# Attention of a fused layer kernel: value sums in a bank of their own, squares a step later, and a new order of input, normalisation and key copies

## The chip, the cores and the metric

One core of a Trainium2 chip runs the kernel. The metric is the device time of one execution in microseconds (us), the median of the runs shown. PE is TensorE, ACT ScalarE, DVE VectorE, POOL GpSimd, SP SyncE.

## The reference

Input is `x` of 64 sequences of 64 tokens with 256 features, and a condition vector of 64 numbers per sequence. Four layers follow each other, all in float32:

```python
x = _L0_cond_ref(x, cond_256, ...)   # conditioned RMS norm, gated GELU, quantised down projection, + x
x = _L1_cond_ref(x, cond_256, ...)   # attention with 16 heads, then SwiGLU
x = _L2_cond_ref(x, cond_256, ...)   # adapter with weights generated per sequence
x = _L3_cond_ref(x, cond_256, ...)   # layer norm with a conditioned bias
```

The change is in the attention half of the second layer:

```python
x = x + a_alpha * _attention(_ada_rmsnorm(x, t, gamma_w, beta_w), W_q, W_k, W_v, W_o)
# _ada_rmsnorm: gamma * x * rsqrt(mean(x * x) + EPS) + beta
attn = softmax(scale * einsum('bnqd,bnkd->bnqk', q, k))
o = einsum('bnqk,bnkd->bnqd', attn, v)
```

## The kernel before

Features lie on the partitions. Float32 products are made of three passes over a high and a low part (`SPLITS`, L45): ACT copies a tensor into its high part, POOL or DVE subtracts that from the tensor to get the low part. Attention works on NA = 16 tiles of 256 tokens (4 sequences). It is a software pipeline written out by hand: each engine has an `attention_body(s)` that is called for step t = s.t, and its parts work on the tile t minus a lag (`s.at(lag)`): lag 0 is the input of the projections, 1 the projections, 2 scores and softmax, 3 the transposed probabilities and the weighted values, 4 the output projection and residual. Engines run ahead of each other only as far as the semaphores `A[...]` let them; on each engine the order of the calls is the order of the work.

`pipeline` (L78) writes out the steps up to t = 8 (`PEELED`, L849), runs t = 9 to 14 in a loop, two steps per turn, and writes out t = 15 and, except on POOL, 16. `plain(s)` (L940) is true from step 9 on, `before_plain(s)` (L944) from step 8 on. Steps 1 to 3 on PE are written out apart from the body (from L1381 on, `a1` to `a3`), as are the last ones, `d0` to `d3` (steps 16 to 19). In the first steps the tail of the first layer still runs in between.

What each engine does in a step, with the names used below:

- **POOL** (L1058): the input in parts (`attention_input`, L169): part 0 multiplies x by its rstd (L182), part 1 multiplies gamma (L186) and adds beta (L188), part 2 subtracts the high part to make the low part (L191); the residual (L1056), which adds the scaled output of lag 4 to x; two normalisations (L1047), which multiply the exponentials by the reciprocal of their sums. In steps up to 8 the order is part 0, 1, 2, residual, norm, norm (in step 3 one norm stands ahead of part 2). From step 9 on it is part 1, residual, part 2, norm, norm, part 0 of the next step; step 8 also ends with part 0 of step 9.
- **PE** (L1286): scores (L1215), first transposes (L1237), output projection (L1281), second transposes (L1237), squares (L1266, only for the first four tiles), keys and queries (both L1156), weighted values (L1254), values (L1191). Transposes wait for the normalisations of the step before. Values go to bank 0 in steps 1 and 2 and from step 8 on, and otherwise share bank 1 with the keys; there they wait for ACT's key copies (`k_done`). The output projection writes bank 0.
- **ACT** (L1500): value copies (L1465 to L1469; in steps up to 8 two of four, the other two are DVE's), copies of the transposes (L1448) and exponentials (L1440) in turn, the high part of the input (L198), key copies (L1476, two per step), query copy (L1485), high part of the attention output (L1491), `rstd` (L1456, L1459) and `square` (L1498) for the first four tiles. The key copies stand behind the high part and the second exponential, but in step 3.
- **DVE** (L1681): value copies (L1670, L1671) in steps up to 8, maxima (L1643) and subtraction (L1647) twice, the scaled output (L1678; from step 9 on between the two pairs), sums (L1655) and reciprocals (L1658) twice, low part of the attention output (L1664).

The squares of the first four tiles give the rstd rows that the SwiGLU part needs first. `square` works at lag 4 at the end of ACT's step, PE's `squares` and ACT's `rstd` at lag 5 in the next one.

Of the kernel before, what the change touches and what calls it, by code (L numbers as in the profile page):

```python
# [831 lines left out]
def layers(nc, io, core, bank, keep, early, adapter_w, base_w, slot_loaded, out):  # L832
# [5 lines left out]
    GTA = GT1  # L838
# [13 lines left out]
    with ExitStack() as c:  # L852
# [73 lines left out]
            return rows.rearrange("p (n b) (g e f) -> p b e n g f", b=2, e=2, f=HD)[:, member, parity]  # L926

        def value_sums(s, member, parity):
            rows = bank[0 if s.first_tile(2) or s.first_tile(3) or plain(s) else 1][L * member:L * (member + 1), :]
            return rows.rearrange("p (n g e f) -> p e n g f", n=2, e=2, f=HD)[:, parity]  # L930

        def pair_of(ap, two):
# [7 lines left out]
        def plain(s):  # L940

            return not isinstance(s.t, int) or s.t > PEELED
# [3 lines left out]
            return not isinstance(s.t, int) or s.t >= PEELED  # L946

        def vector_takes_values(s):
            return not plain(s) or s.last(2)

        def rows_live(s):

# [88 lines left out]
        def _(pool):  # L1041
# [8 lines left out]
            def residual(s):  # L1050
                if s.live(4):
                    t = s.at(4)
                    xt = x[:, :, bass.ds(t * GTA, GTA)]
                    pool.wait_ge(A["ya_done"], t + 1)
                    hold(pool, A["passed"])
                    nc.gpsimd.tensor_tensor(xt, xt, ya1[:], ALU.add).then_inc(A["x_done"], 1)  # L1056

            def attention_body(s):  # L1058
                following = Step(s.t + 1, s.k + 1, NA, s.turns)
                if s.live(0):  # L1060
                    if not plain(s):
                        attention_input(nc, pool, core, s, 0)
                    attention_input(nc, pool, core, s, 1)
                    if s.first_tile(4):
                        first["row_scales"](pool, e35)
                    if plain(s):
                        residual(s)
                    if s.first_tile(3):
                        normalise(s, 0)
                    wait(pool, A["v_ready"], s.at(1) if s.live(2) else 0)  # L1070
                    attention_input(nc, pool, core, s, 2)
                    if not plain(s):
                        residual(s)
                if not s.first_tile(3):
                    normalise(s, 0)
                normalise(s, 1)
                if before_plain(s) and following.live(0):
                    attention_input(nc, pool, core, following, 0)

            def generator_base():  # L1080
                pool.wait_ge(A["base_loaded"], 32)
# [67 lines left out]
        def _(pe):  # L1149
# [19 lines left out]
            def keys(s):  # L1169
                if s.live(1):  # L1170
                    pe.wait_ge(A["h_ready"], s.at(1) + 1)
                    if s.first_tile(3):
                        pe.wait_ge(A["k_done"], s.at(1))
                    elif s.live(2):
                        pe.wait_ge(A["v_low_done"], s.at(1))
                        pe.wait_ge(A["v_high_done"], s.at(1))
                    project(s, W1_K, bank[1], "k_ready")

            def values(s):

                if not s.live(1):
                    return
                k, apart = s.slot(1, 2), s.first_tile(1) or s.first_tile(2) or before_plain(s)
                if before_plain(s):
                    pe.wait_ge(A["ya_done"], s.at(4) + 1)
                elif not apart:
                    pe.wait_ge(A["k_done"], s.at(1) + 1)
                for pair in range(2):
                    for n, (a, b) in enumerate(SPLITS):
                        for d in range(DH):  # L1190
                            last = nc.tensor.matmul(bank[0 if apart else 1][:, pair * D:(pair + 1) * D],  # L1191
                                                    ha[a][k][:, d, pair * P:(pair + 1) * P],
                                                    w1[b][:, W1_V + d * D:W1_V + (d + 1) * D],
                                                    start=n == d == 0, stop=n == 2 and d == DH - 1)
                last.then_inc(A["v_ready"], 1)
# [74 lines left out]
            def output(s):  # L1270
                if s.live(4):
                    ps = output_ps(s)
                    pe.wait_ge(A["ot_done"], s.at(4) + 1)
                    if plain(s) and not s.last(3) and not s.last(4):
                        pe.wait_ge(A["v_low_done"], s.at(2) + 1)
                        pe.wait_ge(A["v_high_done"], s.at(2) + 1)
                    wait(pe, A["ya_done"], s.at(4))
                    for m in range(DH):
                        for n, (a, b) in enumerate(SPLITS):
                            for d in range(2):  # L1280
                                last = nc.tensor.matmul(ps[:, m * GTA:(m + 1) * GTA],  # L1281
                                                        w1[a][:, W1_O + d * D + m * P:W1_O + d * D + (m + 1) * P], ot[b][:, d, :],
                                                        start=n == d == 0, stop=n == 2 and d == 1)
                    last.then_inc(A["o_ready"], 1)

            def attention_body(s):  # L1286
                scores(s)
                transposes(s, 0)
                output(s)
                transposes(s, 1)  # L1290
                squares(s)
                keys(s)
                queries(s)
                weighted_values(s)
                if s.first_tile(4):
                    pe.wait_ge(A["sub_done"], PAIRS * s.at(2) + 1)
                    first["row_lines"](pe, e36)
                values(s)
# [136 lines left out]
        def _(act):  # L1435
# [55 lines left out]
                    nc.scalar.activation(ot[0][:], weighted_ps(s), ACT.Copy).then_inc(A["ot_hi_done"], 1)  # L1491

            def square(s):
                if early(s, 4):
                    act.wait_ge(A["x_done"], s.at(4) + 1)
                    wait(act, A["ss_ready"], s.at(4))
                    hold(act, A["passed"])
                    nc.scalar.activation(sq[:], x[:, :, bass.ds(s.at(4) * GTA, GTA)], ACT.Square).then_inc(A["sq_done"], 1)  # L1498

            def attention_body(s):  # L1500
                take_values(s)
# [6 lines left out]
                exponentials(s, 0)  # L1508
                first_two = s.first_tile(3) or s.first_tile(4)
                take_transposed(s, 1)  # L1510
                if first_two:
                    exponentials(s, 1)
                if s.first_tile(3):
                    take_queries(s)
                if s.live(0):
                    wait(act, A["v_ready"], s.at(1) if s.live(2) else 0)
                    attention_input_high(nc, act, core, s.at(0), s.slot(0, 2))
                if not first_two:
                    exponentials(s, 1)
                if not s.first_tile(3):  # L1520
                    take_keys(s)
                    take_queries(s)
                output_high(s)
                if s.first_tile(4):
                    first["take_lines"](act, e37)
                rstd(s)
                square(s)

            def gate(s, f):
                u = s.at(1) * FC + f  # L1530
# [655 lines left out]
```

## Time and profile before

| | us |
|---|---|
| median of 3 runs (lowest, highest) | 741.57 (741.37, 742.21) |
| the profiled execution | 741.11 |
| its span, first to last instruction | 739.3 |
| busy: PE, DVE, POOL, ACT | 721.8, 514.7, 410.6, 359.3 |
| attention part, on PE's timeline | about 226 to 391 |

The profile is one execution. Times in it count from the start of its span. The granted TensorE clock is 0.998 of full over the whole span. A timeline row has the start in us, the duration in us, engine, line, operation, out<-in, shape, count, and in brackets how long the engine was idle before it and what released it. A row x2 covers two instructions back to back. The end of an instruction overlaps the start of the next by some hundredths, so the distance of two starts is the cost of one.

### The profile page before, as it was taken

How to read it: one execution, taken by the hardware profiler on the slowest of the kernel's cores; microseconds unless marked ns; L12 is line 12 of the kernel's file. 1: busy time of each engine (PE TensorE's matmuls, PEld its weight loads, DVE VectorE, ACT ScalarE, POOL GpSimd, SP SyncE). 2: the span in 40 equal slices, each digit the busy share in tenths (PEclk: the TensorE clock that was granted, in tenths of full speed). 3: DMA queues.
4: the chain of work that ended last, by engine and by line, in shares of the span. 5: the costliest groups of instructions: out<-in, count | busy, mean ns of one | idle time of the engine just before them, and what ended most of it. 6: DMA issues, size and time to landing. Idle time of an engine off the chain costs nothing.

```text
span 739.3 us, 18704 instructions
## 1 busy us (share of the span) xinstructions
PE 721.8 (98%) x6700; PEld 586.4 (79%) x6700; DVE 514.7 (70%) x808; ACT 359.3 (49%) x722; POOL 410.6 (56%) x408
## 2 busy tenths in 40 slices
PE   9999999999999899999999999999999999999996
PEld 8888888888888788888888777777777767778884
DVE  4977777777789989888995465656655566453466
ACT  4534444344447677888874333333333332322585
POOL 5645655554678888999997624224242423320244
PEclk9999999999999999999999999999999999999999
DMA  8854544445432000000004255577667777759943
GB/s 301 258 111 99 108 121 101 100 111 121 110 73 63 22 28 17 17 1 0 1 4 134 104 173 175 177 220 216 191 190 251 212 215 231 238 160 390 386 178 142
DMA packets 81339, 106.25 MB, mean 144 GB/s; under 512 B 39904, under 2 KB 53376, under 8 KB 81152
## 3 DMA queue, kind: packets, MB, share of 16 engines
q1 hardware_dynamic: 79840, 103.34, 46.7%
q10 hardware_dynamic: 1440, 2.11, 1.1%
q8 instruction: 39, 0.64, 0.4%
q14 instruction: 20, 0.16, 0.1%
HBM read 75.77 MB, written 21.27 MB: 131 GB/s over the span
## 4 chain that ended last, share of the span: by engine, by line
PE 75%; POOL 16%; issue 5%; DVE 3%; ACT 1%; DMA 0%; POOLq 0%; DVEq 0%; SPq 0%; ACTq 0%
PE banks L446 24%; PE banks L1317 22%; PE banks L1347 12%; POOL p_sb L1047 5%; PE banks L1369 4%; PE banks L530 4%; POOL mlp_in L182 2%; PE banks L1979 2%; PE banks L1949 2%; POOL mlp_in L186 2%; POOL x_sb L1056 2%; POOL att_in_lo L191 1%; PE banks L1971 1%; POOL mlp_in L188 1%; PE banks L548 1%
## 5 line engine op out<-in xcount | busy, mean ns | idle before, releaser
L629 ACT ACTIVATE gelu<-banks,rstd 128x512 f32<-128x512 f32 x64 | 44.0, 688 | 115.8 <-PE banks L446 114.1
L1699 DVE TENSOR_TENSOR g<-banks,silu 128x512 f32<-128x512 f32 x64 | 44.2, 690 | 77.6 <-PE banks L1317 44.9
L1703 DVE TENSOR_TENSOR g_lo<-g,g_hi 128x512 fp32r<-128x512 f32 x64 | 55.7, 870 | 47.6 <-ACT g_hi L1539 47.6
L1539 ACT ACTIVATE g_hi<-g 128x512 fp32r<-128x512 f32 x64 | 40.4, 631 | 96.0 <-DVE g L1699 95.0
L1533 ACT ACTIVATE silu<-banks 128x512 f32<-128x512 f32 x64 | 38.2, 597 | 97.4 <-PE banks L1317 97.4
L446 PE MATMUL banks<-up_hi,xs_hi 128*128 128x512 f32 x254 | 81.1, 400 | 0.0
L446 PE MATMUL banks<-up_hi,xs_lo 128*128 128x512 f32 x256 | 79.2, 391 | 0.0
L1317 PE MATMUL banks<-mlp_in_hi,w_hi 128*128 128x512 f32 x252 | 78.8, 394 | 0.0
L446 PE MATMUL banks<-up_lo,xs_hi 128*128 128x512 f32 x256 | 78.8, 390 | 0.0
L1317 PE MATMUL banks<-mlp_in_lo,w_hi 128*128 128x512 f32 x252 | 78.0, 390 | 0.0
L1317 PE MATMUL banks<-mlp_in_hi,w_lo 128*128 128x512 f32 x252 | 77.8, 390 | 0.0
L745 DVE SCALAR_TENSOR_TENSOR h<-banks,rstd,gelu 128x512 f32<-128x512 f32 x64 | 47.8, 747 | 37.0 <-ACT gelu L629 37.0
L822 POOL TENSOR_TENSOR mlp_in_lo<-mlp_in,mlp_in_hi 128x1024 fp32r<-128x1024 f32 x8 | 19.9, 2490 | 80.7 <-ACT mlp_in_hi L829 80.7
L1047 POOL TENSOR_TENSOR p_sb<-p_sb,rec 128x1024 f32<-128x1024 f32 x32 | 60.4, 1906 | 5.2 <-DVE rec L1658 5.2
L446 PEld LDWEIGHTS banks<-up_hi,xs_lo 128*128 128x128 f32 x256 | 48.1, 188 | 10.4
L446 PEld LDWEIGHTS banks<-up_lo,xs_hi 128*128 128x128 f32 x256 | 48.1, 188 | 10.2
L1317 PEld LDWEIGHTS banks<-mlp_in_lo,w_hi 128*128 128x128 f32 x252 | 47.3, 188 | 10.7
L1317 PEld LDWEIGHTS banks<-mlp_in_hi,w_hi 128*128 128x128 f32 x252 | 47.2, 188 | 10.8
L1317 PEld LDWEIGHTS banks<-mlp_in_hi,w_lo 128*128 128x128 f32 x252 | 47.3, 188 | 10.2
L1347 PE MATMUL banks<-g_hi,w_hi 128*128 128x512 f32 x128 | 52.6, 411 | 0.7 <-DVE g_lo L1703 0.7
L446 PEld LDWEIGHTS banks<-up_hi,xs_hi 128*128 128x128 f32 x254 | 45.4, 188 | 8.3 <-issue 0.2
L1347 PE MATMUL banks<-g_hi,w_lo 128*128 128x512 f32 x128 | 50.6, 395 | 0.0
(230 smaller groups left out, 1736.2 us busy)
## 6 DMA issues: line engine op xcount, KB each, us to landing
gen_hyper<-in_gen_t SPq DMA_DIRECT2D x32, 512.0 KB, 4.4
gen_made<-base_w SPq DMA_DIRECT2D x64, 256.0 KB, 4.4
adapter_w<-gen_made SPq DMA_DIRECT2D x64, 256.0 KB, 4.4
tokens<-in_x_tok SPq DMA_DIRECT2D x32, 128.0 KB, 2.3
w_stage<-in_w_t SPq DMA_DIRECT2D x32, 128.0 KB, 2.6
tokens_again<-in_x_tok SPq DMA_DIRECT2D x32, 128.0 KB, 2.2
weight_slot<-adapter_w SPq DMA_DIRECT2D x4, 1024.0 KB, 8.8
x_sb<-in_x_t SPq DMA_DIRECT2D x7, 512.0 KB, 6.3
```

The costliest lines, as they stand in the source:

```text
L446: last = nc.tensor.matmul(up_bank(s, j, part)[:, :], (xs_hi, xs_lo)[a][:, k, d, :], up[b][:, d, at:at + 512], start=start and d == 0, stop ...
L530: last = nc.tensor.matmul(y_ps, qt[:, s.slot(2, 2), f, :], downq[:, f, :], start=f == 0, stop=f == FC - 1)
L629: nc.scalar.activation(gelu[:, j, :], up_bank(s, j, 1)[:, :], ACT.Gelu, scale=rstd0[:, bass.ds(s.at(0), 1)]).then_inc(Z["gelu_done"], 1)
L745: nc.vector.scalar_tensor_tensor(out=h[:, k, j * 512:(j + 1) * 512], in0=up_bank(s, j, 0)[:, :], scalar=rstd0[:, bass.ds(t, 1)], in1=gelu[ ...
L1047: nc.gpsimd.tensor_tensor(pu, pu, rec[:, two, :].unsqueeze(2).to_broadcast([P, 16, L]), ALU.mult).then_inc(A["norm_done"], 1)
L1317: last = nc.tensor.matmul(chunk_bank(s, f, i)[:, :], w1[a][:, at:at + P], hs[b][k][:, d, :], start=n == d == 0, stop=n == 2 and d == DH - 1)
L1347: last = nc.tensor.matmul(bank[5 + m][:, :], w1[a][:, at:at + P], gs[b][:, f % 2, :], start=f == n == 0, stop=f == FC - 1 and n == 2)
L1369: last = nc.tensor.matmul(ps[B * half:B * (half + 1), :], scaled[rows, :], hyper[rows, k, half, :], start=True, stop=True)
L1533: nc.scalar.activation(silu[:, f % 2, :], chunk_bank(s, f, 0)[:, :], ACT.Silu).then_inc(S["silu_done"], 1)
L1539: nc.scalar.activation(gs[0][:, f % 2, :], g[:, f % 2, :], ACT.Copy).then_inc(S["g_hi_done"], 1)
L1699: nc.vector.tensor_tensor(g[:, f % 2, :], chunk_bank(s, f, 1)[:, :], silu[:, f % 2, :], ALU.mult).then_inc(S["g_done"], 1)
L1703: nc.vector.tensor_tensor(gs[1][:, f % 2, :], g[:, f % 2, :], gs[0][:, f % 2, :].bitcast(FP32), ALU.subtract).then_inc(S["g_ready"], 1)
```

## The change

Four things. (1) Values always go to bank 0. They wait for the scaled output of lag 4 (from step 4 on), and in steps 2 and 3 for the value copies of the tile before; keys wait for the key copies of the tile before and no longer for value copies; the output projection now waits for the value copies in steps 4 to 8 too. From step 3 on ACT makes all four value copies (DVE keeps its two in step 2 and in the last one). (2) `square` moves to lag 5 and to the place behind ACT's second transposed copy; on PE `squares` moves behind the queries. (3) On ACT, from step 9 on, the key copies stand ahead of the high part of the input. (4) On POOL the residual stands ahead of part 2 in steps 5 to 8 as well; in step 3 both norms stand ahead of part 2, in step 4 the first norm ahead of it and the second behind it, ahead of the residual; from step 8 on, part 0 of the next step stands between the two norms.

```diff
--- before.py
+++ after.py
@@ -926,7 +926,7 @@
             return rows.rearrange("p (n b) (g e f) -> p b e n g f", b=2, e=2, f=HD)[:, member, parity]
 
         def value_sums(s, member, parity):
-            rows = bank[0 if s.first_tile(2) or s.first_tile(3) or plain(s) else 1][L * member:L * (member + 1), :]
+            rows = bank[0][L * member:L * (member + 1), :]
             return rows.rearrange("p (n g e f) -> p e n g f", n=2, e=2, f=HD)[:, parity]
 
         def pair_of(ap, two):
@@ -946,7 +946,7 @@
             return not isinstance(s.t, int) or s.t >= PEELED
 
         def vector_takes_values(s):
-            return not plain(s) or s.last(2)
+            return s.first_tile(2) or s.last(2)
 
         def rows_live(s):
 
@@ -1057,25 +1057,31 @@
 
             def attention_body(s):
                 following = Step(s.t + 1, s.k + 1, NA, s.turns)
+                first_two = s.first_tile(3) or s.first_tile(4)
                 if s.live(0):
                     if not plain(s):
                         attention_input(nc, pool, core, s, 0)
                     attention_input(nc, pool, core, s, 1)
                     if s.first_tile(4):
                         first["row_scales"](pool, e35)
-                    if plain(s):
+                    if not first_two:
                         residual(s)
+                    if first_two:
+                        normalise(s, 0)
                     if s.first_tile(3):
-                        normalise(s, 0)
+                        normalise(s, 1)
                     wait(pool, A["v_ready"], s.at(1) if s.live(2) else 0)
                     attention_input(nc, pool, core, s, 2)
-                    if not plain(s):
+                    if s.first_tile(4):
+                        normalise(s, 1)
+                    if first_two:
                         residual(s)
-                if not s.first_tile(3):
+                if not first_two:
                     normalise(s, 0)
-                normalise(s, 1)
                 if before_plain(s) and following.live(0):
                     attention_input(nc, pool, core, following, 0)
+                if not first_two:
+                    normalise(s, 1)
 
             def generator_base():
                 pool.wait_ge(A["base_loaded"], 32)
@@ -1169,26 +1175,24 @@
             def keys(s):
                 if s.live(1):
                     pe.wait_ge(A["h_ready"], s.at(1) + 1)
-                    if s.first_tile(3):
+                    if s.live(2):
                         pe.wait_ge(A["k_done"], s.at(1))
-                    elif s.live(2):
-                        pe.wait_ge(A["v_low_done"], s.at(1))
-                        pe.wait_ge(A["v_high_done"], s.at(1))
                     project(s, W1_K, bank[1], "k_ready")
 
             def values(s):
 
                 if not s.live(1):
                     return
-                k, apart = s.slot(1, 2), s.first_tile(1) or s.first_tile(2) or before_plain(s)
-                if before_plain(s):
+                k = s.slot(1, 2)
+                if s.live(4):
                     pe.wait_ge(A["ya_done"], s.at(4) + 1)
-                elif not apart:
-                    pe.wait_ge(A["k_done"], s.at(1) + 1)
+                elif s.live(2):
+                    pe.wait_ge(A["v_low_done"], s.at(1))
+                    pe.wait_ge(A["v_high_done"], s.at(1))
                 for pair in range(2):
                     for n, (a, b) in enumerate(SPLITS):
                         for d in range(DH):
-                            last = nc.tensor.matmul(bank[0 if apart else 1][:, pair * D:(pair + 1) * D],
+                            last = nc.tensor.matmul(bank[0][:, pair * D:(pair + 1) * D],
                                                     ha[a][k][:, d, pair * P:(pair + 1) * P],
                                                     w1[b][:, W1_V + d * D:W1_V + (d + 1) * D],
                                                     start=n == d == 0, stop=n == 2 and d == DH - 1)
@@ -1271,7 +1275,7 @@
                 if s.live(4):
                     ps = output_ps(s)
                     pe.wait_ge(A["ot_done"], s.at(4) + 1)
-                    if plain(s) and not s.last(3) and not s.last(4):
+                    if not s.last(3) and not s.last(4):
                         pe.wait_ge(A["v_low_done"], s.at(2) + 1)
                         pe.wait_ge(A["v_high_done"], s.at(2) + 1)
                     wait(pe, A["ya_done"], s.at(4))
@@ -1288,9 +1292,9 @@
                 transposes(s, 0)
                 output(s)
                 transposes(s, 1)
-                squares(s)
                 keys(s)
                 queries(s)
+                squares(s)
                 weighted_values(s)
                 if s.first_tile(4):
                     pe.wait_ge(A["sub_done"], PAIRS * s.at(2) + 1)
@@ -1491,11 +1495,11 @@
                     nc.scalar.activation(ot[0][:], weighted_ps(s), ACT.Copy).then_inc(A["ot_hi_done"], 1)
 
             def square(s):
-                if early(s, 4):
-                    act.wait_ge(A["x_done"], s.at(4) + 1)
-                    wait(act, A["ss_ready"], s.at(4))
+                if early(s, 5):
+                    act.wait_ge(A["x_done"], s.at(5) + 1)
+                    wait(act, A["ss_ready"], s.at(5))
                     hold(act, A["passed"])
-                    nc.scalar.activation(sq[:], x[:, :, bass.ds(s.at(4) * GTA, GTA)], ACT.Square).then_inc(A["sq_done"], 1)
+                    nc.scalar.activation(sq[:], x[:, :, bass.ds(s.at(5) * GTA, GTA)], ACT.Square).then_inc(A["sq_done"], 1)
 
             def attention_body(s):
                 take_values(s)
@@ -1508,23 +1512,26 @@
                 exponentials(s, 0)
                 first_two = s.first_tile(3) or s.first_tile(4)
                 take_transposed(s, 1)
+                square(s)
                 if first_two:
                     exponentials(s, 1)
                 if s.first_tile(3):
                     take_queries(s)
+                if plain(s):
+                    take_keys(s)
                 if s.live(0):
                     wait(act, A["v_ready"], s.at(1) if s.live(2) else 0)
                     attention_input_high(nc, act, core, s.at(0), s.slot(0, 2))
                 if not first_two:
                     exponentials(s, 1)
+                if not plain(s) and not s.first_tile(3):
+                    take_keys(s)
                 if not s.first_tile(3):
-                    take_keys(s)
                     take_queries(s)
                 output_high(s)
                 if s.first_tile(4):
                     first["take_lines"](act, e37)
                 rstd(s)
-                square(s)
 
             def gate(s, f):
                 u = s.at(1) * FC + f
```

## Rows read from the trace of the kernel before

**Rows 1.** The page's chain that ended last, share of the span by engine.

```profile
PE 75%; POOL 16%; issue 5%; DVE 3%; ACT 1%; DMA 0%; POOLq 0%; DVEq 0%; SPq 0%; ACTq 0%
```

**Rows 2.** Windows: length, busy PE, PEld, DVE, ACT, POOL (instructions), clock, DMA.

```profile
...
280.00:290.70 10.70, 10.19 (x226) 9.22 (x225) 9.68 (x13) 8.34 (x15) 9.68 (x9) 1.00 0.09 28
...
331.20:341.20 10.00, 9.61 (x210) 8.79 (x209) 8.80 (x10) 7.99 (x14) 9.62 (x9) 1.00 0.00 0
...
```

**Rows 3.** Timeline of POOL, steps 3 to 6.

```profile
...
245.82 1.91 POOL L1047 TENSOR_TENSOR p_sb<-p_sb,rec 128x1024 f32<-128x1024 f32 x1
...
258.84 1.28 POOL L182 TENSOR_TENSOR mlp_in<-x_sb,stat 128x512 f32<-128x512 f32 x1
...
269.46 1.28 POOL L182 TENSOR_TENSOR mlp_in<-x_sb,stat 128x512 f32<-128x512 f32 x1
...
273.86 1.30 POOL L191 TENSOR_TENSOR mlp_in_lo<-mlp_in,mlp_in_hi 128x512 fp32r<-128x512 f32 x1 [0.87 <-ACT mlp_in_hi L198]
...
```

**Rows 4.** Timeline of POOL, one step of the loop.

```profile
...
332.71 1.04 POOL L186 TENSOR_TENSOR mlp_in<-mlp_in,cond_vectors 128x512 f32<-128x512 f32 x1 [0.20 <-POOL mlp_in L182]
333.94 1.05 POOL L188 TENSOR_TENSOR mlp_in<-mlp_in,cond_vectors 128x512 f32<-128x512 f32 x1 [0.19 <-POOL mlp_in L186]
334.95 1.32 POOL L1056 TENSOR_TENSOR x_sb<-x_sb,y_alpha 128x512 f32 x1
336.23 1.29 POOL L191 TENSOR_TENSOR mlp_in_lo<-mlp_in,mlp_in_hi 128x512 fp32r<-128x512 f32 x1
337.47 3.77 POOL L1047 TENSOR_TENSOR p_sb<-p_sb,rec 128x1024 f32<-128x1024 f32 x2
341.19 1.29 POOL L182 TENSOR_TENSOR mlp_in<-x_sb,stat 128x512 f32 x1
...
```

**Rows 5.** Timeline of PE, starts of groups of matmuls.

```profile
...
220.41 0.48 PE L1156 MATMUL banks<-mlp_in_hi,w_hi 128*128 128x256 f32 x2
...
247.87 0.71 PE L1237 MATMUL banks<-ident,p_sb 64*128 64x64 f32 x16 [0.73 <-POOL p_sb L1047]
...
277.44 1.21 PE L1215 MATMUL banks<-k_sb,q_sb 32*64 32x128 f32 x64
...
286.50 0.51 PE L1191 MATMUL banks<-w_hi,mlp_in_hi 128*128 128x256 f32 x2 [0.51 <-ACT k_sb L1476]
...
371.65 0.71 PE L1237 MATMUL banks<-ident,p_sb 64*128 64x64 f32 x16
...
372.29 0.50 PE L1156 MATMUL banks<-att_in_hi,w_hi 128*128 128x256 f32 x2
...
377.81 1.21 PE L1215 MATMUL banks<-k_sb,q_sb 32*64 32x128 f32 x64
...
```

**Rows 6.** Timeline of ACT.

```profile
...
222.11 1.26 ACT L1476 ACTIVATE k_sb<-banks,vecs 128x512 f32<-128x512 f32 x2 [0.82 <-PE banks L1156]
...
273.08 0.63 ACT L198 ACTIVATE mlp_in_hi<-mlp_in 128x512 fp32r<-128x512 f32 x1 [0.49 <-POOL mlp_in L188]
...
336.51 1.25 ACT L1476 ACTIVATE k_sb<-banks,vecs 128x512 f32<-128x512 f32 x2
337.65 0.60 ACT L1485 ACTIVATE q_sb<-banks 128x512 f32<-128x512 f32 x1
...
338.60 0.38 ACT L1465 ACTIVATE v_sb<-banks 64x256 f32<-64x256 f32 x1
...
```

**Rows 7.** Timeline of DVE, step 7.

```profile
...
278.68 1.22 DVE L1643 TENSOR_REDUCE mx<-banks 128x16 f32<-128x1024 f32 x1 [0.26 <-PE banks L1215]
...
283.46 0.68 DVE L1678 TENSOR_TENSOR y_alpha<-banks,cond_vectors 128x512 f32<-128x512 f32 x1
...
285.30 0.25 DVE L1658 RECIPROCAL rec<-rsum 128x16 f32<-128x16 f32 x1
...
```

**Rows 8.** Timeline of POOL, ends of steps 8 and 15.

```profile
...
297.61 3.77 POOL L1047 TENSOR_TENSOR p_sb<-p_sb,rec 128x1024 f32<-128x1024 f32 x2
...
370.83 2.38 POOL L812 TENSOR_TENSOR mlp_in<-x_sb,stat 128x1024 f32<-128x1024 f32 x1
...
```

## The prediction

> **What bounds the kernel now.** Read the chain of waits first: PE holds 75% of it, POOL 16% [rows 1]. POOL's share all lies in the attention part, 226 to 391 us, so that part is read by windows: in a step of the loop POOL is busy 9.62 of 10.00 us and PE 9.61, DVE and ACT 8.80 and 7.99; in an early step POOL is at 9.68 of 10.70 and PE at 10.19 [rows 2]. Then the timeline of POOL. An early step takes 269.46 - 258.84 = 10.62 us, and 0.87 of it is POOL waiting for ACT's high part of the input before it can subtract the low part [rows 3]. In the loop the residual stands in that hole; what is left is 0.20 before gamma and 0.19 before beta, each waiting for the instruction just ahead on POOL [rows 4]. From the end of the second normalisation of step 8 (297.61 + 3.77 = 301.38) to the start of the SwiGLU input (370.83) lie seven steps, 69.45 us, 9.92 each [rows 8]. Behind that point POOL is on the chain until PE takes over, and everything later follows, so a shift there goes to the end of the kernel whole.
>
> **The change, part by part.** Write E(t) for the end of the second normalisation of step t, T1(t) for PE's second transposes, S(t) for its scores.
>
> *Steps 3 and 4.* Two value copies leave DVE for ACT, where they are of the kind in [rows 6] (0.38 us, some 0.39 apart); the maxima start about 0.9 earlier, with scores already there, and reciprocals and normalisations follow. I take 0.88. The first two norms now run ahead of low part and residual; POOL's work is only reordered, so the input of step 5 starts at 258.84 - 0.88 = 257.96 [rows 3]. PE gains more (its transposes and keys no longer stand behind the low part): T1(5) about 257.3.
>
> *Steps 5 to 8.* The residual covers the 0.87 hole, so POOL alone would need 10.62 - 0.9 = 9.72. But PE was busy 10.19 of 10.70 [rows 2], its hole being the 0.51 before the values, which waited for the key copies [rows 5]. Values in bank 0 lose that wait; squares only change place. PE then needs 10.1. At the turn to step 6 it pays once more. ACT starts the high part when beta ends (261.5), and with the exponential (1.0), key copies (1.14) and query copy its queries are there some 3.3 later, 264.8, where PE could take scores at 263.9: 0.9. Then high output, two rstd activations and four value copies run to 267.4, and the output matmuls, which write that bank, could have gone at 266.7: 0.7. So T1(6) = 257.3 + 10.1 + 1.6 = 269.0 and, with ACT now ahead, T1(7) = 279.1. Scores follow T1 by 377.81 - 371.65 = 6.16 [rows 5], with the squares 6.5; the scaled output ends 1.24 + 5.46 us after the scores start (277.44, 278.68, 283.46 + 0.68) [rows 5, 7]. So S(8) = 285.7, the scaled output of step 8 is there at 292.4, and POOL goes on without a hole: residual 1.28, low part 1.24, first norm 1.86, next input 1.28 (taken like the residual, same form), second norm 1.9 [rows 4]: E(8) = 300.0, 1.4 earlier than 301.38.
>
> *Steps 9 to 14, the loop.* Here POOL's order becomes gamma, beta, residual, low, norm, next input, norm. On POOL by itself this is a gain: the second norm stands between the next input and gamma, and about 0.2 of the 0.4 us of gaps goes, 9.92 to 9.73. What is pushed back is T1: it waits for the second norm, which now ends 1.28 later in the step. And ACT now copies the keys ahead of the high part. Keys on PE stand behind T1. So a loop of one step closes, all links from rows without cover:
> - second norm to T1: 247.87 - 245.82 = 2.05 (PE had waited for it) [rows 3, 5];
> - T1 to keys 0.64 [rows 5];
> - keys to the first key copy 222.11 - 220.41 = 1.70 (ACT had waited) [rows 5, 6];
> - two key copies 337.65 - 336.51 = 1.14 [rows 6];
> - high part to low part 273.86 - 273.08 = 0.78 (POOL had waited) [rows 3, 6];
> - low part 1.24, first norm 3.72 / 2 = 1.86, next input 1.28 [rows 4].
>
> The sum is 10.69 us per step against 9.92. Of the parts, keys first costs nothing while T1 is early (T1 lay 0.7 before gamma), nor does the moved input while keys come last; the cover of each is what the other takes. Put on POOL's clock: keys are copied by E + 3.6 and the high part by E + 4.3, where POOL wants it at E + 3.5. Six such steps are 64.14, and step 15 has no next input, 10.69 - 1.28 = 9.41: 73.55 against 69.45, a loss of 4.1. No register wait or loop branch is added that the loop of before does not have; I bound the sum of links between 10.4 (each hand-over 0.05 shorter, as POOL to ACT looks in the loop) and 10.9 (each 0.03 longer).
>
> *Free of cost.* DVE's two copies less per early step (it is not the bound); keys' wait for the value copies gone, replaced by one for the older key copies; the square one step later: it is read only by squares that already ran in that step, and waits for a residual of the step before. If ACT were full there, its 0.6 would delay the high part; it has over 1 us idle. No DMA is moved; rstd rows leave in the same step as before.
>
> Sum: -1.4 + 4.1 = +2.7 on the profiled execution's own 741.11 (span 739.30 and 1.8 around it), 743.8. The median of the runs is 741.57, 0.46 above that execution; on the median: **744.2**.
>
> **A rule against this.** By occupancy POOL and PE share the top of a loop step at 9.6 of 10.0 [rows 2]. The Trainium skill (Perfetto Trace Analysis, Identifying the Most-Contended Engine) says the engine with the highest occupancy is the one to improve, and the change does fill POOL's gaps. The row agrees about who is fullest; it does not say what fills the step once the order changes. Followed by itself, that rule gives rival 1.
>
> **Rivals.**
> 1. *Faster: the key copies do not hold the high part.* If keys were ready early enough, the next bound of the loop is a cycle over two steps: norm to T1 2.05, T1 to scores 6.16, to maxima 1.24, maxima to reciprocal's end 285.30 + 0.25 - 278.68 = 6.87, 0.07, norm 1.86, input 1.28 = 19.5, so 9.8 each [rows 4, 5, 7]. Then 6 x 9.8 + 8.5 = 67.3, 2.1 less than 69.45, with the 1.4: -3.5, 738.1. It decides at (69.45 + 1.4 + 1.28) / 7 = 10.3 us per loop step: below, faster; above, slower. For it: both saturated engines gain slack. Against: links measured without cover sum to 10.69.
> 2. *PE does not bind in steps 5 to 8*: E(8) = 257.96 + 4 x 9.72 + 1.28 = 298.1, 3.3 gained: +0.8, 742.4. Against it PE's 10.19 busy.
> 3. *No gain in steps 5 to 8*, since ACT's 0.76 of copies hold the output matmuls each step: 10.62 stays, E(8) = 301.7: +4.4, 746.0.
> 4. The reordering is hidden throughout, 741.6.
>
> **How the numbers follow.** Forecast 0.52 (its own range 743.0 to 745.4), rival 1 0.24, rival 2 0.11, rival 3 0.10, rival 4 0.03. A measurement of this kernel tells about 0.2% (1.5 us) from nothing, so rivals 2 and 4 are "same": 0.14. Faster is rival 1, 0.24; slower is forecast and rival 3, 0.62. The range takes forecast, 2, 3 and 4, which is 0.76, and the upper half of rival 1 (loop steps between 9.9 and 10.2): 738.8 to 746.6.
>
> **What the changed profile would show.** POOL's 0.87 hole of steps 5 to 8 gone and PE's wait for key copies before the values too; in the loop the gap before gamma gone, a new POOL wait of 0.8 to 1.0 before the low part, released by ACT's high part, with the key copies just ahead of it on ACT; T1 waiting on POOL; PE idle about 1.1 per step; loop steps 10.7 apart; the SwiGLU input starting at 373.5. I am wrong in the main point if loop steps are under 10.3 apart or that wait is missing; only in size, if E(8) is off 300.0.

## Result and profile after

The changed kernel takes 747.11 us (median of 5, 746.34 to 747.35) against 742.14 for the kernel before on the same chip (median of 5): ratio 1.0073 [1.0062, 1.0085], 5.0 us slower. The forecast was 744.2, in a range of 738.8 to 746.6, or +2.6 on its before (741.57): the side was right, the size 2.4 short. The measured loss added to the forecast's own before would make 746.5, just inside that range.

The page's busy times and its chain by engine, after. POOL's share falls from 16% [rows 1] to 11% and "issue" rises to 8%:

```profile
PE 723.2 (97%) x6700; PEld 587.9 (79%) x6700; DVE 506.4 (68%) x796; ACT 365.9 (49%) x734; POOL 410.4 (55%) x408
...
PE 75%; POOL 11%; issue 8%; DVE 3%; ACT 1%; DMA 0%; POOLq 0%; DVEq 0%; SPq 0%; ACTq 0%
```

The time went in two places, and the timeline of POOL shows both. Each L182 row starts the input of a step (3, 4, 5, 6, 7, 8); 300.68 is the second norm of step 8, 376.27 the SwiGLU input:

```profile
237.78 1.29 POOL L182 TENSOR_TENSOR mlp_in<-x_sb,stat 128x512 f32<-128x512 f32 x1
...
242.54 3.77 POOL L1047 TENSOR_TENSOR p_sb<-p_sb,rec 128x1024 f32<-128x1024 f32 x2 [1.23 <-DVE rec L1665]
...
247.70 1.29 POOL L182 TENSOR_TENSOR mlp_in<-x_sb,stat 128x512 f32<-128x512 f32 x1
...
258.85 1.31 POOL L182 TENSOR_TENSOR mlp_in<-x_sb,stat 128x512 f32<-128x512 f32 x1
...
268.58 1.28 POOL L182 TENSOR_TENSOR mlp_in<-x_sb,stat 128x512 f32<-128x512 f32 x1
...
274.31 1.31 POOL L1056 TENSOR_TENSOR x_sb<-x_sb,y_alpha 128x512 f32<-128x512 f32 x1 [2.21 <-ACT mlp_in_hi L198]
...
280.53 1.31 POOL L182 TENSOR_TENSOR mlp_in<-x_sb,stat 128x512 f32<-128x512 f32 x1
...
290.92 1.28 POOL L182 TENSOR_TENSOR mlp_in<-x_sb,stat 128x512 f32<-128x512 f32 x1
...
300.68 1.93 POOL L1047 TENSOR_TENSOR p_sb<-p_sb,rec 128x1024 f32<-128x1024 f32 x1
...
376.27 2.40 POOL L812 TENSOR_TENSOR mlp_in<-x_sb,stat 128x1024 f32<-128x1024 f32 x1
```

Profiled executions reach the attention part at different times (the input of step 3 starts at 237.38 before and 237.78 here, between 236.65 and 238.30 in all), so stretches are compared from that row on. From it to the SwiGLU input, 133.45 us have become 138.49: +5.04, which is the loss in the medians (4.97).

**The loop.** From the end of step 8's second norm, 302.61, to 376.27 are 73.66 us, where before had 69.45. One step, POOL:

```profile
311.41 1.91 POOL L1047 TENSOR_TENSOR p_sb<-p_sb,rec 128x1024 f32<-128x1024 f32 x1
...
315.51 1.31 POOL L1056 TENSOR_TENSOR x_sb<-x_sb,y_alpha 128x512 f32 x1
317.77 1.29 POOL L191 TENSOR_TENSOR mlp_in_lo<-mlp_in,mlp_in_hi 128x512 fp32r<-128x512 f32 x1 [0.96 <-ACT mlp_in_hi L198]
319.02 1.90 POOL L1047 TENSOR_TENSOR p_sb<-p_sb,rec 128x1024 f32<-128x1024 f32 x1
320.88 1.27 POOL L182 TENSOR_TENSOR mlp_in<-x_sb,stat 128x512 f32 x1
322.12 1.90 POOL L1047 TENSOR_TENSOR p_sb<-p_sb,rec 128x1024 f32<-128x1024 f32 x1
```

The timeline of PE and that of ACT in the same step:

```profile
313.47 0.71 PE L1241 MATMUL banks<-ident,p_sb 64*128 64x64 f32 x16 [0.77 <-POOL p_sb L1047]
314.11 0.50 PE L1162 MATMUL banks<-att_in_hi,w_hi 128*128 128x256 f32 x2
```

```profile
315.91 1.27 ACT L1480 ACTIVATE k_sb<-banks,vecs 128x512 f32<-128x512 f32 x2 [0.67 <-PE banks L1162]
317.07 0.63 ACT L198 ACTIVATE mlp_in_hi<-mlp_in 128x512 fp32r<-128x512 f32 x1
```

This is a closed ring: each step waits for the step before through all of the links. POOL's norm, begun at 311.41, lets PE's second transposes go at 313.47 (2.06); keys follow 0.64 later; ACT copies them 1.80 after that, then makes the high part (1.16); POOL's low part starts at 317.77 (0.70), and after low part, norm and input (1.25, 1.86, 1.24) the next second norm starts at 322.12: 10.71. POOL was ready 0.96 before the high part came, where before it had no wait [rows 4].

**Steps 6 to 8.** Step 6 lasts 11.95 (268.58 to 280.53), where before took 10.61. PE and ACT at its start:

```profile
264.13 0.40 PE L1195 MATMUL banks<-w_hi,mlp_in_lo 128*128 128x256 f32 x2
266.56 2.02 PE L1219 MATMUL banks<-k_sb,q_sb 32*64 32x128 f32 x64 [2.03 <-ACT early_rstd L1460]
268.50 1.11 PE L1241 MATMUL banks<-ident,p_sb 64*128 64x64 f32 x16
```

```profile
265.13 0.59 ACT L1489 ACTIVATE q_sb<-banks 128x512 f32<-128x512 f32 x1
265.60 0.60 ACT L1495 ACTIVATE ot_hi<-banks 128x512 fp32r<-128x512 f32 x1
266.08 0.33 ACT L1460 ACTIVATE early_rstd<-banks,wscale 128x64 f32<-128x64 f32 x1
```

The scores write bank 3, where the sums of squares lie until the first rstd activation has read them. ACT comes to that activation only behind key copies, queries and high output, so PE waits on it (`ss_done`). It was no earlier before: 7.20 after the input of step 5 (266.04 - 258.84), now 7.23 (266.08 - 258.85). The same place in the kernel before, ACT and PE:

```profile
266.04 0.33 ACT L1456 ACTIVATE early_rstd<-banks,wscale 128x64 f32<-128x64 f32 x1
```

```profile
265.25 0.50 PE L1191 MATMUL banks<-w_hi,mlp_in_hi 128*128 128x256 f32 x2 [0.69 <-ACT k_sb L1476]
...
266.87 1.21 PE L1215 MATMUL banks<-k_sb,q_sb 32*64 32x128 f32 x64
```

There PE's values had stood for the key copies, and its scores started at 266.87, when the activation was over (266.37). Values in bank 0 no longer stand for them; PE is through with the values at 264.53 and meets what lay hidden behind that wait. The new place of the squares on PE has no part in it: they are done at 262.03, 4 us ahead of the activation. The scores then took 2.02 where 1.21 was usual [rows 5]. A window of both, and the loop step (columns as in [rows 2]):

```profile
266.50:268.60 2.10, 2.04 (x66) 1.74 (x68) 0.43 (x1) 1.66 (x5) 2.10 (x3) 0.50 0.00 0
...
323.98:334.69 10.71, 9.87 (x208) 8.99 (x208) 8.95 (x11) 8.31 (x14) 9.55 (x8) 1.00 0.00 0
```

After the 2.03 us of idle PE was granted 0.50, its 1.2 GHz level, until about 269.9. So the scaled output is late and POOL stands 2.21 before the residual at 274.31. (The row names ACT's high part, which had long been done; DVE's scaled output, 273.45 to 274.13, came last.) PE's largest entry of waits in steps 5 to 8, with the sum, the number and the longest:

```profile
PE banks L1219 <- ACT early_rstd L1460: 3.1, 3, 2.0
```

### The profile page after: what moved, and what is told of

It reads as the page before. It is cut to its first block, busy times and chain, and to the rows that moved or that the text cites. A ratio compares the mean times of both kernels' runs of the same rounds, so it can differ in the third digit from the quotient of the medians.

```text
span 745.3 us, 18706 instructions
## 1 busy us (share of the span) xinstructions
PE 723.2 (97%) x6700; PEld 587.9 (79%) x6700; DVE 506.4 (68%) x796; ACT 365.9 (49%) x734; POOL 410.4 (55%) x408
## 4 chain that ended last, share of the span: by engine, by line
PE 75%; POOL 11%; issue 8%; DVE 3%; ACT 1%; DMA 0%; POOLq 0%; DVEq 0%; SPq 0%; ACTq 0%
PE banks L446 24%; PE banks L1321 22%; PE banks L1351 12%; PE banks L1373 4%; PE banks L530 4%; POOL p_sb L1047 2%; PE banks L1986 2%; PE banks L1956 2%; POOL mlp_in L182 2%; POOL x_sb L1056 2%; POOL mlp_in L186 1%; DVE mx L1650 1%; POOL mlp_in_lo L191 1%; PE banks L1978 1%; PE banks L548 1%
## 5 line engine op out<-in xcount | busy, mean ns | idle before, releaser
L1710 DVE TENSOR_TENSOR g_lo<-g,g_hi 128x512 fp32r<-128x512 f32 x64 | 52.4, 819 | 47.5 <-ACT g_hi L1546 47.5
L1321 PEld LDWEIGHTS banks<-mlp_in_lo,w_hi 128*128 128x128 f32 x252 | 47.3, 188 | 10.7
L1321 PEld LDWEIGHTS banks<-mlp_in_hi,w_lo 128*128 128x128 f32 x252 | 47.3, 188 | 10.3
```

The costliest lines, as they stand in the source:

```text
L1321: last = nc.tensor.matmul(chunk_bank(s, f, i)[:, :], w1[a][:, at:at + P], hs[b][k][:, d, :], start=n == d == 0, stop=n == 2 and d == DH - 1)
L1710: nc.vector.tensor_tensor(gs[1][:, f % 2, :], g[:, f % 2, :], gs[0][:, f % 2, :].bitcast(FP32), ALU.subtract).then_inc(S["g_ready"], 1)
```

## Experiments

Each kernel was timed against the kernel before on its own chip, whose median was 741.44 in the first four, 741.50 in the next four and 741.49 in the last two; beside the changed kernel it was 742.14, so that kernel is compared with them by its distance to before, +5.0. Two theories stood against each other: that the two late edits (next input between the norms, keys first) together close the loop and the early part merely falls short; or that one of them is bad by itself.

### Next input behind both norms

```diff
@@ attention_body (POOL), from the changed kernel
                 if not first_two:
                     normalise(s, 0)
-                if before_plain(s) and following.live(0):
-                    attention_input(nc, pool, core, following, 0)
                 if not first_two:
                     normalise(s, 1)
+                if before_plain(s) and following.live(0):
+                    attention_input(nc, pool, core, following, 0)
```

> Edit: the changed kernel, but on POOL the input of the next step goes back behind both normalisations; keys stay first on ACT. My theory (the loss is a loop of one step: second norm, T1, keys, key copies, high part, low part, norm, input; 10.7 us): with T1 early again the key copies are done before beta ends, keys first costs nothing, loop steps are 9.9 apart, no wait before the low part; the whole 5.4 us of steps 8 to 15 come back, about 741.8, within 0.5 of the kernel before. Rival 'keys first alone holds the high part': steps stay at 10.5 or more, 746 to 747.

741.19, ratio 0.9995 [0.9986, 1.0005]. POOL:

```profile
313.65 1.32 POOL L1056 TENSOR_TENSOR x_sb<-x_sb,y_alpha 128x512 f32 x1
314.92 1.29 POOL L191 TENSOR_TENSOR mlp_in_lo<-mlp_in,mlp_in_hi 128x512 fp32r<-128x512 f32 x1
...
323.60 1.29 POOL L1056 TENSOR_TENSOR x_sb<-x_sb,y_alpha 128x512 f32 x1
```

The wait before the low part is gone and the step is 9.95, though keys are still copied ahead of the high part.

### Keys last on ACT

```diff
@@ attention_body (ACT), from the changed kernel
-                if plain(s):
-                    take_keys(s)
...
-                if not plain(s) and not s.first_tile(3):
-                    take_keys(s)
                 if not s.first_tile(3):
+                    take_keys(s)
                     take_queries(s)
```

> Edit: the changed kernel, but on ACT the key copies go back behind the high part and the second exponential; the input stays between the norms on POOL. My theory: the one-step loop is open, so the next bound holds: POOL alone at 9.73 or the cycle over two steps at 9.8. Steps 9 to 14 at 9.75 to 9.95, the part behind 301 us about 1 us shorter than in the kernel before: 740.3 to 741.5. Rival 'the moved input alone does it, since T1 is pushed back': steps 10.5 or more, 746 to 747.

741.65, ratio 1.0004 [0.9993, 1.0015]. POOL:

```profile
313.23 1.31 POOL L1056 TENSOR_TENSOR x_sb<-x_sb,y_alpha 128x512 f32 x1
...
316.11 1.91 POOL L1047 TENSOR_TENSOR p_sb<-p_sb,rec 128x1024 f32<-128x1024 f32 x1 [0.32 <-DVE rec L1662]
...
323.30 1.30 POOL L1056 TENSOR_TENSOR x_sb<-x_sb,y_alpha 128x512 f32 x1
```

The median is 0.15 above the expected range. With the keys out of the way the waits that are left are where rival 1 put them, on the reciprocals: the norm waits 0.32 for them in this step and 0.22 in the next, and residuals lie 9.72, 10.07 and 9.96 apart (from 303.51), where rival 1 had 9.8.

### Both undone: the early part alone

Both diffs above together.

> Edit: the changed kernel with both late edits undone (input behind both norms, keys last); what is left is the early part: values apart, squares later, the order of steps 3 to 8. My theory as the changed trace now shows it: the early part is worth nothing (end of step 8 at 302.6 less the 1.24 of the moved input is 301.4, as before), so 741.8 plus or minus 0.6, loop steps 9.9. What I predicted of it (1.4 us faster) would give 740.5. Rival 'the early part costs itself, through the waits for rstd': 743 or more.

740.83, ratio 0.9992 [0.9982, 1.0001]: 0.4 under the expected range. So the whole early part is worth 0.6 us, not clear of nothing, and not the 2.6 that the forecast holds for it (step 8 ends 1.4 earlier there although the moved input, 1.28, already stands ahead of its end; the 740.5 of the expectation left the 1.28 out). PE, and a window of its clock:

```profile
265.44 1.20 PE L1219 MATMUL banks<-k_sb,q_sb 32*64 32x128 f32 x64 [2.08 <-ACT early_rstd L1460]
```

```profile
266.50:268.60 2.10, 2.10 (x30) 1.92 (x22) 1.90 (x2) 1.64 (x3) 2.10 (x2) 0.59 0.00 0
```

### The late part alone

The kernel before, with only the two late edits of the change (keys first on ACT in the loop, next input between the norms).

> Edit: the kernel before with the two late edits alone (from step 8 the input between the norms, from step 9 keys first). My theory: 5.4 us slower than before, 747, loop steps 10.7, with a wait of 1.0 before the low part. Rival 'late and early parts hurt together': under 744.

747.23, ratio 1.0074 [1.0058, 1.0091], no different from the changed kernel. POOL:

```profile
315.60 1.31 POOL L1056 TENSOR_TENSOR x_sb<-x_sb,y_alpha 128x512 f32 x1
317.86 1.29 POOL L191 TENSOR_TENSOR mlp_in_lo<-mlp_in,mlp_in_hi 128x512 fp32r<-128x512 f32 x1 [0.95 <-ACT mlp_in_hi L198]
...
326.29 1.31 POOL L1056 TENSOR_TENSOR x_sb<-x_sb,y_alpha 128x512 f32 x1
```

Steps of 10.69 to 10.71 us. The two edits together cost 5.8 us (on top of the early part 5.6: +5.0 less -0.6), each alone nothing that these runs tell (0.4 and 0.8 above the kernel with neither, intervals overlapping): the loop needs both to close. That settles the late part. The next four kernels ask where the early gain went. All start from the kernel with both late edits undone (740.83).

### Squares back at their earlier place

```diff
@@ square (ACT); likewise squares ahead of keys on PE
-                if early(s, 5):
-                    act.wait_ge(A["x_done"], s.at(5) + 1)
+                if early(s, 4):
+                    act.wait_ge(A["x_done"], s.at(4) + 1)
...
                 take_transposed(s, 1)
-                square(s)
...
                 rstd(s)
+                square(s)
```

> Edit, on the kernel with both late edits undone (input and keys last): the square part of the change undone too (ACT squares at lag 4 at the end of its step, PE's squares ahead of the keys). The residual of tile 0 is now the last thing POOL does in step 4 (it ends at 258.9), so the square at the end of ACT's step 4 would hold ACT from 254.5 until then, in front of the value copies of step 5. Theory: this costs 3 to 4.5 us, 744 to 745.5; the later square is what the new order of steps 3 and 4 needs. Rival 'the later square is what costs (it makes the rstd late)': 740 or less.

746.12, ratio 1.0055 [1.0040, 1.0069]: 5.2 worse than with later squares, more than either expectation. ACT and POOL:

```profile
258.68 0.63 ACT L1502 ACTIVATE sq<-x_sb 128x512 f32<-128x512 f32 x1 [4.80 <-POOL x_sb L1056]
```

```profile
267.07 1.31 POOL L1056 TENSOR_TENSOR x_sb<-x_sb,y_alpha 128x512 f32<-128x512 f32 x1 [5.06 <-DVE y_alpha L1682]
```

The residual now stands behind norms in the first steps; a square that still wants that step's residual stops ACT for 4.80, its value copies behind it, and PE's output matmuls stand 5.08 for these. PE was then granted 0.50 from about 260.0 to 266.9, so the 5.2 are that stop and the clock together; step 5 takes 14.80 instead of 9.70. The later squares are no saving of their own but what the new order needs. Nor is their place on PE what makes the scores wait for rstd, since one such wait is left with the squares ahead of the keys:

```profile
292.58 1.20 PE L1219 MATMUL banks<-k_sb,q_sb 32*64 32x128 f32 x64 [0.31 <-ACT early_rstd L1460]
```

### First rstd activation ahead of the high output

```diff
@@ attention_body (ACT); rstd(s, (0,)) is the first activation, (1,) the second
                 square(s)
+                if s.first_tile(5):
+                    rstd(s)
...
+                if not s.first_tile(5):
+                    rstd(s, (0,))
                 output_high(s)
...
-                rstd(s)
+                if not s.first_tile(5):
+                    rstd(s, (1,))
```

> Edit, on the kernel with both late edits undone: ACT's rstd earlier. In step 5 both activations stand right behind the square, where ACT idles 1.85 us; in steps 6 to 8 the first one, the only one that the scores wait for, stands ahead of the high output, the second behind it. Theory (the early gain was lost at scores that wait for the rstd activation which frees their bank, 2.0 to 2.1 us idle at step 6, 0.4 and 0.7 at the next two, and a lower clock behind the first): scores of step 6 start 0.5 earlier, the two later waits go, PE's idle time before the scores is 1.5 and the clock stays up; 1.0 to 2.0 us faster than with both late edits undone, 738.8 to 739.8. Rival 'queries, not rstd, set the scores': under 0.3 us.

739.42, ratio 0.9976 [0.9967, 0.9984]: 1.5 less against before than without it, and faster than both kernels of this study. PE, step 6:

```profile
265.02 1.20 PE L1219 MATMUL banks<-k_sb,q_sb 32*64 32x128 f32 x64 [1.55 <-ACT k_sb L1482]
```

```profile
266.50:268.60 2.10, 2.10 (x28) 1.90 (x27) 2.07 (x2) 1.37 (x2) 2.10 (x2) 1.00 0.00 0
```

The scores' wait on rstd is gone, the one left in step 6 ends with ACT's query copy (264.33 to 264.92; the row names the key copies, done by then), and the clock stays at 1.00. (In step 5 both activations stand right behind the square, where ACT had been idle.)

### Both rstd activations ahead of it

The same, with `rstd(s)` whole ahead of `output_high(s)`.

> Edit, on the kernel with both late edits undone: both rstd activations ahead of the high output in steps 5 to 8. Theory: the scores of step 6 wait for the query copy and one activation, 0.5 less than now, the high output comes 0.6 later and has room: 0.3 to 1.0 faster than with both late edits undone, 739.8 to 740.5. Rival: high output late holds DVE's low part and the maxima, no gain.

741.26, ratio 0.9992 [0.9983, 1.0001]: no gain. PE:

```profile
266.55 1.20 PE L1219 MATMUL banks<-k_sb,q_sb 32*64 32x128 f32 x64 [1.58 <-ACT early_rstd L1460]
268.24 0.72 PE L1241 MATMUL banks<-ident,p_sb 64*128 64x64 f32 x16 [0.50 <-DVE ot_lo L1668]
```

The high output, now 1.08 behind the query copy instead of 0.48, holds DVE's low output and by it PE: 0.50, 0.46 and 0.46 in three steps. The kernel's one profile is shorter than this median says (131.62 from the input of step 3 to the SwiGLU input, against 132.98 without the edit, in a profile with the clock's fall). Part of the rest is the clock: four of its eleven executions have a mean clock of 0.995 and take 741.41 to 742.35; the median of the other seven is 740.44, against 739.33 for the ten of twelve that kept the clock with only the first activation ahead. The two kernels also differ in step 5, so the last 1.1 us isn't split further.

### DVE takes two of the value copies again

```diff
@@ vector_takes_values; steps 3 to 8 split the four copies as before
-            return s.first_tile(2) or s.last(2)
+            return not plain(s) or s.last(2)
```

> Edit, on the kernel with both late edits undone: DVE takes two of the four value copies again in steps 3 to 8. Theory: maxima of step 3 start 0.9 later (what the change gained there, about 0.6 of it real) but ACT's copies end 0.8 earlier, which bounds only the output matmuls (waits of 0.2 in all): 741.0 to 741.6, 0.2 to 0.6 slower than with both late edits undone. Rival 'four copies on ACT are what ate the early gain' (rival 3 of the prediction): 1 us or more faster, under 740.

741.22, ratio 0.9998 [0.9988, 1.0007]. PE:

```profile
266.13 1.20 PE L1219 MATMUL banks<-k_sb,q_sb 32*64 32x128 f32 x64 [2.13 <-ACT early_rstd L1460]
```

With 0.76 us less on ACT the wait is no shorter: rival 3's cause falls. The first norm of step 3 waits 1.82 again and that step is 10.50 long instead of 9.91, so the moved copies are worth 0.6 in that profile, once.

### The rstd repair with the loop open, and with the loop closed

The rstd diff above, on the kernel with keys last alone, and on the changed kernel itself.

> The key copies of the loop stand behind the high part and the exponential again, the next input stays between the norms, and the first rstd activation of steps 6 to 8 runs ahead of the high output (step 5: both behind the square). My theory: the early repair is worth what it was with both late edits undone, about 1.4 us (739.42 against 740.83), and the loop stays open at steps of 9.7 to 10.1 us, so 741.65 - 1.4 = 740.3, range 739.2 to 741.2; scores of step 6 start near 265.0 with the granted clock near 1.00 behind them. Rival: with keys last the loop follows a two-step cycle through the maxima (about 9.9 us a step) that doesn't care when it is entered, so the gain of the early part is swallowed: 741.4 to 741.9.

> The changed kernel whole, with only the first rstd activation of steps 6 to 8 ahead of the high output (step 5: both behind the square). My theory: the early part and the closed loop of the late steps add up, so the repair is worth its 1.4 us here too and the loop still steps by 10.7 us: 747.1 - 1.4 = 745.7, range 744.9 to 746.3, with the SwiGLU input 1.4 to 1.9 us earlier than 376.27. Rival: the early loss was cover for the loop and the loop absorbs an earlier start: 746.8 to 747.4.

The first: 739.69, ratio 0.9978 [0.9969, 0.9987], as fast as the best, so the loop with keys last passes an early gain on. The second: 744.60, ratio 1.0051 [1.0037, 1.0065], +3.1 against before where the changed kernel has +5.0: 1.9 gained (by the traces 138.49 - 136.53 = 1.96), not 1.4. The 744.60 itself is 0.3 under the bottom of my range, which had not allowed for the other chip's before. Its POOL, the end of step 8 and a loop step:

```profile
298.15 1.92 POOL L1047 TENSOR_TENSOR p_sb<-p_sb,rec 128x1024 f32<-128x1024 f32 x1
...
312.96 1.31 POOL L1056 TENSOR_TENSOR x_sb<-x_sb,y_alpha 128x512 f32 x1
...
323.60 1.29 POOL L1056 TENSOR_TENSOR x_sb<-x_sb,y_alpha 128x512 f32 x1
```

Step 8 ends at 300.07, 2.54 before the changed kernel (0.70 of it because its attention began earlier), and the loop still goes by 10.64: the losses of the two parts add up. With the activation in its new place the changed kernel comes near what was forecast for it (+2.6).

## Why the prediction was right in its side and wrong in its size

**The loop, right.** Forecast: steps of 10.69, a wait of 0.8 to 1.0 before the low part on ACT's high part with the key copies just ahead, 1.1 us of PE idle per step, 73.55 us from E(8) to the SwiGLU input. Measured: 10.70 and 10.71, 0.96, 10.71 - 9.87 = 0.84 idle, 73.66. The ring's links were each within 0.10 of the rows that the forecast took them from. That each edit covers for the other was shown by the two kernels that undo one of them. Taking each link only from rows where the receiver had been waiting, so that nothing hid a part of it, held.

**Steps 3 and 4: 0.88 forecast, 0.39 measured** (input of step 5 at 21.46 us after that of step 3 before, 21.07 after). DVE in step 3:

```profile
235.75 1.16 DVE L1650 TENSOR_REDUCE mx<-banks 128x16 f32<-128x1024 f32 x1
237.43 1.23 DVE L1654 TENSOR_TENSOR p_sb<-banks,mx 128x1024 f32<-128x1024 f32 x1 [0.52 <-PE banks L1241]
```

The maxima did start earlier, by 1.0 against the start of attention (236.36 before), but the subtraction then waited 0.52 for PE's second transposes, which still read its buffer; 0.6 reached the norm, and 0.2 of that went between low part and next input. In step 4 POOL had no wait on another engine in either kernel (11.16 and 11.15 us), so nothing could be gained there.

**Steps 5 to 8: the step that failed.** E(8), the end of step 8's second norm, was put 42.04 after the input of step 5; it came after 302.61 - 258.85 = 43.76, which is 1.72 late. With 0.49 and 0.11 of the other two stretches that is all of the 2.3 us missed (5.04 against 2.7). The term is "at the turn to step 6 it pays once more": the forecast let the scores go when the queries are copied, 3.3 after the start of the high part, with PE idle 0.9. The copy took that long (262.50 to 265.72, 3.22), but the scores started 0.84 behind it, at 266.56. They also wait for the first rstd activation, which frees their bank and stands behind the high output on ACT. The forecast named both activations only as ACT's work ahead of the output matmuls. PE stood 2.03 instead of 0.9, and the clock that it then lost is about 0.87 more: two kernels with nearly the same wait (2.03 and 2.12) and no fall have step 6 at 11.08 instead of 11.95. The wait had not shown in the kernel before because the values' wait for the key copies covered it, and the forecast took that wait away without asking what lay behind it. That the activation's place costs this is shown by the kernel that moves it; what covered it before is read from the rows, and no run puts the key wait back alone. The entry "free of cost" for the squares is not what failed, as the activation comes no later than before.

With the activation ahead of the high output (loop closed) step 8's norm ends 300.07 - 258.16 = 41.91 after the input of step 5, near the 42.04, and the loss is 3.1. That agreement is in part luck: the scores of step 6 then wait 1.55, where the forecast had 0.9 there and 0.7 for output matmuls, which wait for nothing. Against that kernel, steps 6, 7 and 8 of the changed one are 1.44, 0.35 and 0.04 longer.

**The rivals.** Rival 1 (faster) fell in this kernel, as the step of 10.7 is past its 10.3; its two-step cycle fits what is left once keys come last (9.9 to 10.0 instead of 9.8), though no run cut it. Rival 2 fell: step 5 takes its 9.73, but even with the repair step 7 takes 10.04. Rival 3 had nearly the right time, +4.4, for a wrong reason: no gain in steps 5 to 8, but by the rstd wait and not by the value copies. The Trainium skill's rule (Perfetto Trace Analysis, Identifying the Most-Contended Engine) still picks POOL, 9.55 of 10.71 in the window above (for PE, whose headroom that section judges by its weight loads, 8.99), and says nothing of the 10.71 itself, which is a sum of links over four engines.

## What to carry to other kernels

Two reorderings that are each free can close a ring together; add up the ring with both in place, with links from rows where the receiver was waiting, and compare the sum with the step. When a wait is taken away, list everything else that the engine's next instruction needs, buffers as well as data, and when each is there: something that was always late may have been hidden behind the wait. A short activation that frees a bank belongs ahead of longer ones that nobody waits for yet; here, taking its partner along, which frees no bank, gave the gain back in the medians.

## What the runs showed of the hardware that was not expected

An idle stretch of about 2 us inside a busy part can cost TensorE its clock, and doesn't always. Ahead of the scores of step 6 PE stood 2.03 (the changed kernel) and 2.08 (early part alone) and was then granted 0.50 for some 3 us. In the changed kernel that began at the end of the idle stretch, in the other only about 1.4 us after it, so that its scores still took 1.20. With waits of 2.03, 2.12 and 2.13 in the first, second and eighth kernel the rows stay at 1.00, as they do after 1.55 and 1.58. One profile each does not tell what decides.

The mean clocks of all executions say how often. The kernel before was never under 0.997 in the 69 executions timed beside the ten kernels; its longest wait on PE is 1.2. A mean of 0.995 or 0.996, which fits one such fall (half the clock for some 3 of 740 us), comes in 15 of the 46 executions of the five kernels with a wait of 2.0 to 2.1 (four of the changed kernel's five, none of the ten of the kernel with the next input behind both norms) and in 7 of the 39 with about 1.6. So the repair makes the fall rarer and does not end it, and a part of each difference of medians above is how many executions fell. The same repair gave 1.9 us on the changed kernel and 1.5 with both late edits undone.
